# Second attention of a two-layer network: head products in their own 64 rows, scores of one head beside those of another

## The reference, cut to what matters

```python
q = (x @ wq).reshape(B, S, 16, 16).transpose(0, 2, 1, 3)
k = (x @ wk).reshape(B, S, 4, 16).transpose(0, 2, 1, 3)
v = (x @ wv).reshape(B, S, 4, 16).transpose(0, 2, 1, 3)
q = q * cos + _rotate_half(q) * sin
k = k * cos + _rotate_half(k) * sin
scores = jnp.einsum('bhqd,bhkd->bhqk', q, repeat(k, 4)) / sqrt(16)
scores = jnp.where(causal, scores, -jnp.inf)
out = jnp.einsum('bhqk,bhkd->bhqd', softmax(scores), repeat(v, 4))
x = x + out.transpose(0, 2, 1, 3).reshape(B, S, D) @ wo
```

## Time and profile before

| | us |
|---|---|
| median of 3 runs | 3474.27 (3473.16 to 3474.42) |
| profiled execution, time | 3471.95 |
| profiled execution, span | 3470.2 |
| PE, DVE, ACT, POOL busy | 3213.3, 2348.2, 2064.0, 1184.7 |
| second attention, set-up | 2253 to 2311 |
| its loop, eight sequences, to the last weighting | 2311.3 to 2786 |

### The profile page before, as it was taken

One profiled execution on the slowest core, in us unless ns is written; L12 is line 12 of the kernel. 1 busy time (PEld: TensorE's weight loads), 2 busy tenths in 40 slices (PEclk: granted clock), 3 DMA queues, 4 the chain that ended last, 5 costly groups with the idle time before them and its releaser, 6 DMA issues. The chain is left out here.

```text
span 3470.2 us, 74087 instructions
## 1 busy us (share of the span) xinstructions
PE 3213.3 (93%) x22696; PEld 2398.4 (69%) x22696; DVE 2348.2 (68%) x6849; ACT 2064.0 (59%) x4943; POOL 1184.7 (34%) x1818
## 2 busy tenths in 40 slices
PE   4999999999999999989999979979999964999995
PEld 3777777676777677768888865546666653888884
DVE  5888887887888788776666655556666626666664
ACT  4777777777777777765555543236566621555553
POOL 4434344444333434443333320042321202334432
PEclk9999999999999999999999999969999967999998
DMA  3222222222222222243333331111111134445545
GB/s 95 59 54 59 52 51 57 59 58 54 59 59 54 58 59 57 55 136 121 131 127 127 133 121 49 39 40 28 32 28 27 27 123 148 118 125 143 128 120 164
DMA packets 175948, 280.43 MB, mean 81 GB/s; under 512 B 32850, under 2 KB 117586, under 8 KB 175826
## 3 DMA queue, kind: packets, MB, share of 16 engines
q1 hardware_dynamic: 161234, 258.94, 26.1%
q0 software_dynamic: 14592, 19.93, 3.5%
HBM read 159.79 MB, written 41.16 MB: 58 GB/s over the span
## 5 line engine op out<-in xcount | busy, mean ns | idle before, releaser
L767 POOL TENSOR_SCALAR at_p<-at_p,at_recip 128x128 f32<-128x128 f32 (+3 forms) x1028 | 533.6, 532 | 868.0 <-DVE at_recip L900 868.0
L815 ACT ACTIVATE at_p<-at_p,at_nmax 128x128 f32<-128x128 f32 (+3 forms) x1030 | 573.6, 557 | 336.4 <-DVE at_nmax L894 324.7
L894 DVE CUSTOM_DVE_ANT_0 at_p<-at_s_ps,at_bias 128x128 f32<-128x128 f32 (+3 forms) x1030 | 497.3, 483 | 208.5 <-PE at_s_ps L1031 199.7
L1031 PE MATMUL at_s_ps<-at_k_twice,at_q 64*128 64x128 f32 (+3 forms) x3090 | 379.4, 350 | 5.2 <-DVE at_nmax L894 4.2
L1860 DVE CUSTOM_DVE_ANT_0 aa_a_ps<-aa_a_ps,aa_hidden 128x128 f32<-128x128 f32 (+3 forms) x512 | 247.2, 507 | 173.6 <-PE aa_a_ps L2024 170.8
L1031 PEld LDWEIGHTS at_s_ps<-at_k_twice,at_q 64*128 64x128 f32 x3090 | 232.2, 185 | 176.7 <-issue 162.7
L1052 PE MATMUL at_o_ps<-at_pT,at_v 128*64 128x512 f32 (+3 forms) x2064 | 306.8, 439 | 0.0
L1760 ACT ACTIVATE aa_pT<-aa_b_ps 128x512 f32<-128x512 f32 (+1 forms) x384 | 196.6, 529 | 175.9 <-PE aa_b_ps L2042 173.1
L526 DVE SCALAR_TENSOR_TENSOR nw_hl<-nw_h,nw_coef_now,nw_hh 128x512 fp32r<-128x512 f32 x192 | 149.8, 780 | 163.1 <-ACT nw_hh L454 163.1
L449 ACT ACTIVATE nw_h<-nw_h_ps,nw_b 128x512 f32<-128x512 f32 x192 | 132.1, 688 | 211.1 <-PE nw_h_ps L553 210.6
L905 DVE COPY at_pT<-at_t_ps 128x128 f32<-128x128 f32 (+3 forms) x512 | 248.9, 486 | 0.0
(11 more groups left out here) (317 smaller groups left out, 7942.7 us busy)
## 6 DMA issues: line engine op xcount, KB each, us to landing
at_k_twice<-at_k_parts SPq DMA_DIRECT2D x260, 256.0 KB, 3.7
w_raw<-in_w_dram SPq DMA_DIRECT2D x57, 768.0 KB
nw_w_raw<-in_w_all_dram SPq DMA_DIRECT2D x26, 1024.0 KB, 5.0
nw_w_raw<-in_w_all_dram SPq DMA_DIRECT2D x52, 512.0 KB, 6.8
nw_xh<-xh_dram SPq DMA_DIRECT2D x10, 512.0 KB, 4.3
nw_xl<-xl_dram SPq DMA_DIRECT2D x10, 512.0 KB, 4.9
at_w_raw<-in_w_heads_dram SPq DMA_DIRECT2D x18, 256.0 KB, 4.4
nw_x<-in_x_dram SPq DMA_DIRECT2D x9, 512.0 KB, 5.9
```

The source lines that it names most:

```text
L767: pool.tensor_scalar(p, p, recip[:, u:u + 1], 1.0, ALU.mult, ALU.mult).then_inc(scaled, 1)
L815: act.activation(p_sb[:, u, 0:N], p_sb[:, u, 0:N], ACT.Exp, bias=nmax[:, u:u + 1], scale=-1.0, accum_out=total[:, u:u + 1]).then_inc(exped, 1)
L894: dve.tensor_tensor_reduce(out=p_sb[:, u, 0:N], in0=s_ps[u % 2][:, 0:N], in1=bias[:, u % 2, S - N:S], scale=1.0, scalar=BIG, op0=ALU.add, ...
L1031: ins = pe.matmul(s_ps[h][:, 0:N], qst[par][rows, q, at], k_twice[par][rows, k, 0:N], start=(i == 0), stop=(i == 2))
```

## The change

Each head's products use only its own 64 rows of q and k. `k_all` has one copy of each key head, filled by one ScalarE instruction over all 128 rows (the spread gives both halves alike); its rows of ones come from the bias of that instruction (`one_rows`, made by GpSimd, 1 in rows 48, 49, 112 and 113), so the clears and the 16 DMAs go. The scores of a step, two groups ahead, belong to the other head of the pair (`h ^ 1`), so that they lie in the other half of rows, and each follows the piece of the same width: pieces 0, 1, 2, 3 with scores 3, 2, 1, 0. The closing products become `hide`, after two pieces and after four. Parts are now block 0, block 1, and blocks 3 and 2 together (512, 384, 384 columns). The table of side jobs is moved: `x0` and `x1` are made in steps 14 and 15 two sequences ahead (`AFTER_NEXT`, and before the loop for sequence 1), `q0`, `kk`, `q1` come earlier, `k0` moves to the end of step 4, `p1` and `out0` change slots, and two of the scalings `make_xr` move from steps 14 and 15 to 12 and 13. The masks follow the order 3, 2, 1, 0, also ahead of the loop. Left out below are the new tensor `one_rows`, the two semaphores that go with their waits, and the loops that turn the order of the masks ahead of the loop and in each step.

```diff
@@ -1458,7 +1458,9 @@
-BLOCK_AT = [0, S + P, 2 * S, S]
+PART_AT = [0, S, S + 3 * P]
+PART_COLS = [S, 3 * P, 3 * P]
+BLOCK_AT = [0, S, S + 4 * P, S + 3 * P]
@@ -1520,13 +1522,12 @@
-        ones = turn1[P // 2:P // 2 + QD, 2, :]
...
-        k_all = [sb(f"aa_k{i}", [P, 2, KV1, S], F32R) for i in range(2)]
+        k_all = [sb(f"aa_k{i}", [P, KV1, S], F32R) for i in range(2)]
@@ -1576,11 +1576,12 @@
-        NEXT = {(0, 0): "x0", (0, 1): "x1", (1, 1): "q0", (2, 0): "kk", (2, 1): "q1", (3, 1): "v", (4, 0): "k0",
-                (6, 1): "p0", (7, 1): "p1", (8, 1): "p2", (9, 1): "k1", (10, 0): "p3", (11, 0): "k2", (12, 0): "p4",
+        NEXT = {(0, 1): "q0", (1, 1): "kk", (2, 0): "q1", (3, 1): "v", (4, 1): "k0",
+                (6, 1): "p0", (7, 0): "p1", (8, 1): "p2", (9, 1): "k1", (10, 0): "p3", (11, 0): "k2", (12, 0): "p4",
...
-        BEFORE = {(7, 0): "out0", (8, 0): "out1"}
+        AFTER_NEXT = {(14, 1): "x0", (15, 1): "x1"}
+        BEFORE = {(7, 1): "out0", (8, 0): "out1"}
@@ -1589,11 +1590,13 @@
+            if at in AFTER_NEXT and n + 2 < B:
+                return n + 2, AFTER_NEXT[at]
...
-        ORDER = [(0, name) for name in FIRST]
+        ORDER = [(0, name) for name in FIRST] + [(1, "x0"), (1, "x1")]
@@ -1624,12 +1627,6 @@
-            sp.wait_ge(consts, 4)
-            for i in range(2):
-                for e in range(2):
-                    at = 64 * e + M_ROW
-                    for g in range(KV1):
-                        sp.dma_start(k_all[i][at:at + QD, e, g, :].bitcast(F32), ones).then_inc(ones_placed, 16)
@@ -1696,22 +1692,17 @@
-            pool.wait_ge(consts, 1)
-            pool.memset(ones, 0.0).then_inc(consts, 1)
+            pool.memset(one_rows[:], 1.0).then_inc(consts, 1)
...
-            pool.memset(pT[0][:, :, 0:S], 0.0).then_inc(cleared, 1)
...
-            pool.wait_ge(consts, 3)
-            pool.memset(ones[0:2, :], 1.0).then_inc(consts, 1)
+            pool.affine_select(out=one_rows[:], in_=one_rows[:], compare_op=ALU.is_ge, fill=0.0, base=-M_ROW,
+                               pattern=[[-64, 2]], channel_multiplier=1).then_inc(consts, 1)
...
-
-            for i in range(2):
-                for e in range(2):
-                    pool.wait_ge(cleared, 2 * i + e + 1)
-                    other = slice(64 - 64 * e, P - 64 * e)
-                    pool.tensor_copy(k_all[i][other, e, :, :], pT[0][other, :, 0:S]).then_inc(cleared, 1)
-            pool.wait_ge(cleared, 5)
+            pool.affine_select(out=one_rows[:], in_=one_rows[:], compare_op=ALU.is_ge, fill=0.0, base=M_ROW + 1,
+                               pattern=[[64, 2]], channel_multiplier=-1).then_inc(consts, 1)
+            pool.wait_ge(consts, 5)
+            pool.tensor_tensor(one_rows[:, 0:1], one_rows[:, 0:1], one_rows[:, 1:2], ALU.add).then_inc(consts, 1)
@@ -1753,19 +1744,17 @@
-                N = S if piece < 2 else S // 2
+                at, N = PART_AT[piece], PART_COLS[piece]
...
-                act.activation(pT[group_of(n, s) % 2][:, s % REP, piece * S:piece * S + N], b_ps[done % 3][:, 0:N], ACT.Exp, scale=-1.0)\
+                act.activation(pT[group_of(n, s) % 2][:, s % REP, at:at + N], b_ps[done % 3][:, 0:N], ACT.Exp, scale=-1.0)\
...
-                for e in range(2):
-                    row = slice(64 * e, 64 * e + M_ROW)
-                    ins = act.activation(k_all[n % 2][row, e, g, :], bank_of(n, f"k{g}")[row, :], ACT.Copy)
-                ins.then_inc(act_out, 1)
+                act.activation(k_all[n % 2][:, g, :], bank_of(n, f"k{g}")[:], ACT.Identity, bias=one_rows[:, 0:1])\
+                    .then_inc(act_out, 1)
@@ -1807,7 +1796,11 @@
+                if name == "k0":
+                    act.wait_ge(consts, 6)
...
+            take((1, "x0"))
+            take((1, "x1"))
@@ -1854,11 +1847,12 @@
-                done = (G * REP + h) * TT + i
+                done = (G * REP + h) * TT + TT - 1 - i
...
+                head = h ^ 1
...
-                dve.tensor_tensor_reduce(out=a_ps[i % 2][:, 0:N], in0=a_ps[i % 2][:, 0:N], in1=hidden[:, S - N:S], scale=1.0,
-                                         scalar=BIG, op0=ALU.add, op1=ALU.min, accum_out=nmax[:, G % 2, i, h:h + 1])\
+                dve.tensor_tensor_reduce(out=a_ps[done % 2][:, 0:N], in0=a_ps[done % 2][:, 0:N], in1=hidden[:, S - N:S], scale=1.0,
+                                         scalar=BIG, op0=ALU.add, op1=ALU.min, accum_out=nmax[:, G % 2, i, head:head + 1])\
@@ -1933,13 +1927,13 @@
-                        for i in range(2, TT):
+                        for i in (1, 0):
...
-                    if s in (9, 10, 14, 15) and n + 2 < B:
-                        make_xr(n + 2, (9, 10, 14, 15).index(s))
+                    if s in (9, 10, 12, 13) and n + 2 < B:
+                        make_xr(n + 2, (9, 10, 12, 13).index(s))
@@ -1962,7 +1956,7 @@
-                if name == "kk":
+                if name == ("q0" if n > 0 else "kk"):
@@ -2012,33 +2006,38 @@
-                head = g * REP + h
+                rows = slice(64 - 64 * (h % 2), P - 64 * (h % 2))
+                pair = 2 * g + h // 2
...
-                done = (G * REP + h) * TT + i
-                if h == 0 and i == 0:
+                done = (G * REP + h) * TT + TT - 1 - i
+                if h == 0 and i == 3:
...
-                if h == 2 and i == 0:
+                if h == 2 and i == 3:
...
-                pe.matmul(a_ps[i % 2][:, 0:N], q_all[n % 2][:, head // 2, N - P:N], k_all[n % 2][:, head % 2, g, 0:N],
+                pe.matmul(a_ps[done % 2][:, 0:N], q_all[n % 2][rows, pair, N - P:N], k_all[n % 2][rows, g, 0:N],
...
-            def piece(n, s, part):
+            def piece(n, s, k):
...
-                head = g * REP + h
+                rows = slice(64 * (h % 2), 64 * (h % 2) + 64)
+                pair = 2 * g + h // 2
+                part = min(k, 2)
...
-                if h == 0 and part == 0:
+                if h == 0 and k == 0:
...
-                if done >= 3:
+                if done >= 3 and k < 3:
...
-                blocks = (((0, 0),), ((1, P), (3, 0)), ((2, 0),))[part]
-                for k, at in blocks:
-                    pe.matmul(b_ps[done % 3][:, at:at + S - k * P], k_all[par][:, head % 2, g, k * P:k * P + P],
-                              q_all[par][:, head // 2, k * P:S], start=(k < 3), stop=False)
-                N = len(blocks) * P
+                at, N = BLOCK_AT[k] - PART_AT[part], S - k * P
+                pe.matmul(b_ps[done % 3][:, at:at + N], k_all[par][rows, g, k * P:k * P + P],
+                          q_all[par][rows, pair, k * P:S], start=(k < 3), stop=False)
+
+            def hide(n, s, part):
+                done = (n * STEPS1 + s) * PIECES + part
+                N = P if part < 2 else 2 * P
@@ -2081,18 +2080,18 @@
-            pe.wait_ge(cleared, 5)
-            pe.wait_ge(ones_placed, 16 * 4 * KV1)
...
-                for i in range(TT):
+                for i in (3, 2, 1, 0):
...
-                for i in range(TT):
+                for i in (3, 2, 1, 0):
...
+            side((1, "x0"))
+            side((1, "x1"))
@@ -2100,11 +2099,13 @@
-                        score(G + 2, h, 0)
-                    side(side_job(n, s, 0))
+                        score(G + 2, h, 3)
...
-                        score(G + 2, h, 1)
+                        score(G + 2, h, 2)
+                    hide(n, s, 0)
+                    hide(n, s, 1)
+                    side(side_job(n, s, 0))
@@ -2112,12 +2113,14 @@
-                        score(G + 2, h, 2)
+                        score(G + 2, h, 1)
+                    piece(n, s, 3)
+                    if ahead:
+                        score(G + 2, h, 0)
+                    hide(n, s, 2)
...
-                    if ahead:
-                        score(G + 2, h, 3)
```

More of the change, by code:

```diff
@@ L1540, in attention_phase @@
         twice = sb("aa_twice", [P, 2, P], F32R)
+        one_rows = sb("aa_one_rows", [P, 2])
         a_ps = [ps(f"aa_a_ps{i}") for i in range(2)]
@@ L1549, in attention_phase @@
         consts = sem("aa_consts")
-        cleared = sem("aa_cleared")
-        ones_placed = sem("aa_ones_placed")
         set_up = sem("aa_set_up")
@@ L1689, in _ @@
             sp.wait_ge(tables_loaded, 48)
-            sp.wait_ge(ones_placed, 16 * 4 * KV1)
             sp.wait_ge(placed, 16 * REP * GROUPS)
@@ L1908, in _ @@
             low_k(0)
-            dve.wait_ge(consts, 4)
+            dve.wait_ge(consts, 3)
             dve.tensor_copy(late[:], hidden[:, S - P:S]).then_inc(set_up, 1)
             for h in range(REP):
-                for i in range(TT):
+                for i in (3, 2, 1, 0):
                     mask(0, h, i)
@@ L1927, in _ @@
                     if G + 2 < GROUPS:
-                        for i in range(2):
+                        for i in (3, 2):
                             mask(G + 2, h, i)
```

## The result

The changed kernel takes 3501.55 us (median of 4 runs, 3500.07 to 3506.94), the kernel before on the same chip 3474.35 us: a ratio of 1.0082, 95% interval 1.0064 to 1.0099. The change costs 27 us. The forecast was 3469 us, the range 3448 to 3488: both wrong, and the sign with them.

The account below looks back on a forecast made before the run. TensorE was taken to bound the second attention, the score-mask chain close behind. Terms -4.9 - 0.3 + 2.2 - 0.3 + 0 = -3.3 us, taken as -5, from median 3474.27 gave 3469 us; 8-in-10 range 3448 to 3488.

Parts of the forecast that it names:

- The walk of the steps: Second attention loop: lengths reckoned for each of a sequence's sixteen steps, summing to 60.4 us against 61.2 before.
- parts 1 to 3: Second attention steps: products paired side by side (could save 0.64 us), shape changes at 0.21 us each, scores at the mask chain.
- Part 3: Second attention: scores in twos at VectorE's mask chain, with side jobs; -0.8 us a sequence, six times, -4.9 us.
- half clock in every sequence: Rival, chance 0.17: mask waits bring TensorE to 1.2 GHz once a sequence, 2.2 us each, six more +13: 3482 us.
- +2.2 predicted: Last eight steps of the loop: no scores to pair with, yet shape changes still paid; together +2.2 us.
- four sequences with the same wait keep a full clock: Argument against the half-clock rival: in the loop before, four sequences had step 4's wait yet no lower clock.
- Set-up: Ahead of the loop: sooner start without clears and DMAs -2 us, waiting for x0 and x1 +2 us, together 0.
- the key copies and constants: One ScalarE copy for two lies under TensorE, bias constant made on POOL at the start: 0 us.
- step 4 at 5.3: Sign in the profile after: step 4 of a sequence takes 5.3 us, mask 3 behind the low part of k.
- a sequence over 62.5 us: Sign the forecast is wrong, as is under 59 us: shapes have another price, or an unseen wait ends last.
- Pairs don't overlap: Rival, chance 0.08: score stands at its mask while its partner has gone; +0.3 us on 120 steps, 3505 us.
- pairs at full value: Rival, chance 0.05: shapes cost nothing, TensorE's step base 0.9 us instead of 1.67; -45 us, giving 3425 us.

Follow-up runs that it names:

- e1: The changed kernel plus 17 overwritten 128-row products of 512 columns a sequence, before the second block of seven steps: 3477.09 us, ratio 1.0014.
- e4: The changed kernel with both products of a pair in the same 64 rows, so nothing runs side by side: 3632.86 us, ratio 1.0441.
- e13: The changed kernel with VectorE's low part of k moved ahead of the taking of v in step 3: 3488.57 us, ratio 1.006.
- e6: Same as e1, but its filler products use only 64 rows, with the same columns and count: 3476.02 us.
- e2: The changed kernel's order and side jobs, but 128-row products on two key copies with zero halves, no pairs: 3478.64 us, ratio 1.0015.
- e3: The kernel before with only the moved side jobs of the change: 3473.78 us, ratio 1.0002.
- e7: The kernel before, order and table untouched, each score product reading only its head's 64 rows: 3829.69 us, ratio 1.1041.
- e11: The changed kernel with five 128-row filler products of 512 columns a sequence, four in step 4 and one in step 12: 3494.60 us.
- e12: Same as e11, but the five filler products a sequence use only 64 rows: 3507.27 us.
- e5: Same as e1, with more fillers in the last sequence, ahead of the loop and before the last output projection: 3485.97 us, ratio 1.0044.

## Why the prediction was wrong

**The walk of the steps was right in sum.** With the clock up, in the profile after or in e1, a step takes: 0 to 3, 5.17, 4.60, 4.22 and 4.45 us (walk 5.12, 4.65, 4.5, 4.25); 4 to 7, 5.2, 2.88, 3.03 and 4.28 (5.3, 3.24, 2.9, 4.17); 8 to 11, 4.67, 3.12, 2.84 and 2.72 (4.66, 3.24, 3.0, 2.44); 12 to 15, 3.66, 3.12, 3.28 and 2.88 (3.65, 3.24, 3.15, 2.9). The sum is 60.2 against 60.4, and parts 1 to 3, the pairs, 0.21 us for a change of shape and the mask chain, fit the traces. Single steps are off by up to 0.36 us (step 5), and that these errors cancel is luck. A pair does save what e4 loses; the shapes take it back.

**The step that failed is the one under all the others: that the clock stays as it was.** Part 3 multiplied steps at full clock by six and left the falls to a rival. That rival, half clock in every sequence, had the mechanism and the sign, at 0.17. It was undersized in three ways. It priced one fall a sequence at 2.2 us; there are two in four of the six sequences, and against 60.2 us the six sequences are 385.2 - 6 x 60.2 = 24 us over, 4.0 each (set against the 61.9 of the kernel before on average, 13.6). It had no fall in the last sequence, which costs 12.9 us. Of these, 3.0 are the shapes, against +2.2 predicted: e13's last eight steps, with the clock up until the last of them, take 41.6 us for 38.6. The clock takes most of the rest: without fillers in these steps, the last sequence is 6.5 us shorter in e13 and 8.6 in e6. And it had no further fall in sequence 0, which costs 4.1 us; e1 gives back 3.4 of them, but e6 none.

Its counter-argument, "four sequences with the same wait keep a full clock", was the error in reasoning. It took the wait as what decides. The kernel before has that wait with products of all rows around it; the change keeps the wait and halves the rows of 2560 columns a step. In four of six sequences the clock is down before the wait begins. e13 takes the wait away and keeps a loop at 0.90; e2 keeps the wait, restores the rows, and has 0.97. e2 also takes the changes of shape away, so by itself it does not tell the two apart. The Trainium skill's "TensorE: Matmul & The Clock Gate" (Part 1: The HAM clock gate) ties the clock to how busy the engine has been. The trace does not agree if busy means products in flight. Step 3 of sequence 4 is busy for 4.32 of 4.45 us at full clock, and the clock falls behind it; step 4 of sequence 2 in the kernel before is busy for only 3.22 of 5.03 us and keeps clock 1.00.

**Set-up: predicted 0, measured +4.0.** The sooner start came: first exchange 3 us earlier, first score 24.9 us into the phase for 28.1. From the first score to the loop it is 37.2 us for 30.0, where I had +2 for x0 and x1. e3 has 32.6 (x0 and x1: +2.5), e2 34.4 (the scores' order, masks in the open: +1.8), so 2.8 come with the half rows. Reading half rows ahead of the loop, most of it at half clock, was left out of the sum. e7 shows part of it by itself: half rows in the old order take this stretch from 30.0 to 31.9 us. That it is the changes of shape of the 32 scores there no run shows.

**Right:** the key copies and constants cost nothing that the traces show; step 4 at 5.3 (5.2 in e1) with mask 3 behind the low part of k; pairs within 0.01 us. The prediction also named its own sign of being wrong, a sequence over 62.5 us; all six are. "Pairs don't overlap" is refuted by e4, "pairs at full value" by 60.2 us. **What stays open:** why the clock falls at steps 4 and 12 in particular, and how rows, columns and emptied time weigh against each other for it. Step 3 ends with products of only 64 columns; that they lead to the fall at step 4 no run shows. Nor has any run the change with fewer changes of shape and without a new wait. e11 and e12 speak for it that rows count, not by what rule.

## What to carry over

Before taking rows or columns away from an engine whose clock is granted by its work, ask what the clock will do: price every stretch at both levels, and do not take over a full clock that was seen with products of more rows. A busy share of 93% before and after tells nothing of it; the clock column by sequence does. To tell such a loss from a wait, add work that is thrown away: if the kernel gets faster and the clock column rises, it was the clock.

## What the runs showed of the hardware

Adding 17 overwritten products of 512 columns a sequence saved 24 us (e1). Half-row products alone, at the same columns, cost 10% of the whole kernel (e7), 0.7 to 1.5 us a step with the clock up, in emptying at shape changes, and the rest by the clock. With no wait for a mask over 0.23 us in it, step 4 of sequence 4 still ran at clock 0.53 (e13). A float32 product on plain tiles is issued as two (forty for twenty, 0.43 us each, e5). Between products of 64 rows and of 128 the next weight load starts later (e7): 0.25 us after a 128-column product starts, 0.31 after a 256-column one, for 0.12 within one shape.
